# The norm's weights of queries and keys multiplied into the rotation's tables, first 16-head stage

## The reference, cut to what matters

```python
def rmsnorm(x, w, eps=1e-06):
    v = jnp.mean(x * x, axis=-1, keepdims=True)
    return w * (x * jax.lax.rsqrt(v + eps))

h = modulate(rmsnorm(x, norm1_w), sh_msa, sc_msa)
qkv = (h @ qkv_w.T).reshape(B, N, 3, H, D)          # H = 16, D = 16
q = rmsnorm(q, q_norm_w)                            # weights: 16 values for q, 16 for k
k = rmsnorm(k, k_norm_w)
q_r, k_r = apply_rope3d(q[..., :12], k[..., :12], positions)   # pairs (t0, t1) ->
                                                    # (t0*cos - t1*sin, t0*sin + t1*cos)
q = jnp.concatenate([q_r, q[..., 12:]], axis=-1)    # values 12 to 15 are not rotated
k = jnp.concatenate([k_r, k[..., 12:]], axis=-1)
attn = softmax(einsum("bnhd,bmhd->bhnm", q, k) * D ** -0.5)
x = x + g_msa * (einsum("bhnm,bmhd->bnhd", attn, v) @ proj_w.T + proj_b)
```

## Time and profile before

| | |
|---|---|
| median of 3 runs | 2146.8 us (2143.79 to 2148.41) |
| the profiled execution | 2146.22 us, its span 2144.4 us |
| busy shares of the span | PE 89%, DVE 62%, ACT 46%, POOL 38% |
| mean granted clock of TensorE | 0.958 of full speed |
| layer 1's attention | from 856.4 to about 1194 us of the span |

### The profile page before, as it was taken

How to read it: one execution, slowest core, us unless ns; L and a number is a source line. 1 busy time by engine, 2 the same in 40 slices (tenths; PEclk the granted TensorE clock), 3 DMA queues, 4 the chain that set the end, 5 groups by cost and what they waited for, 6 DMA issues and landing times. The chain is left out here.

```text
span 2144.4 us, 44671 instructions
## 1 busy us (share of the span) xinstructions
PE 1917.3 (89%) x17318; PEld 1484.1 (69%) x17318; DVE 1335.8 (62%) x2028; ACT 995.1 (46%) x1693; POOL 819.1 (38%) x731
## 2 busy tenths in 40 slices
PE   6999999999979997788878899978999799988898
PEld 4777777877867775566666677756777677766675
DVE  4454555455545554698888577767988655554455
ACT  3433443444346665455555333324555466643222
POOL 1220211021113444677778233456778633340000
PEclk8999999999989999799998999989999999998999
DMA  5100000000020000100000000010000000003222
GB/s 192 59 2 2 2 2 2 2 2 2 2 65 1 0 0 3 43 2 3 2 1 1 27 0 0 0 40 2 2 0 2 6 25 0 0 12 101 82 70 79
DMA packets 26172, 44.97 MB, mean 21 GB/s; under 512 B 3984, under 2 KB 11984, under 8 KB 25872
## 3 DMA queue, kind: packets, MB, share of 16 engines
q1 hardware_dynamic: 24720, 42.26, 5.9%
q10 hardware_dynamic: 1280, 0.23, 0.1%
HBM read 36.18 MB, written 6.29 MB: 20 GB/s over the span
## 5 line engine op out<-in xcount | busy, mean ns | idle before, releaser
L1203 DVE TENSOR_TENSOR Glb<-Gfb,Ghb 128x512 fp32r<-128x512 f32 x176 | 165.2, 948 | 97.6 <-ACT Ghb L1154 95.9
L441 PE MATMUL bank<-HH,W1b 128*128 128x512 f32 x448 | 184.8, 412 | 16.1 <-PEq L1483 7.2
L323 POOL TENSOR_TENSOR Tm<-Dv,MOD 128x512 f32<-128x512 f32 x94 | 108.5, 1174 | 228.1 <-DVE Dv L380 157.2
L443 PE MATMUL bank<-HH,W1b 128*128 128x512 f32 x448 | 177.1, 395 | 0.0
L442 PE MATMUL bank<-HL,W1b 128*128 128x512 f32 x448 | 176.8, 395 | 0.0
L441 PE MATMUL O<-Ghb,W2b 128*128 128x512 f32 x352 | 143.0, 406 | 36.7 <-DVE Glb L1203 36.7
L461 POOL TENSOR_TENSOR spare<-RT 128x1 f32<-128x1 f32 x32 | 6.5, 202 | 404.3 <-DVE RT L452 404.3
L312 POOL TENSOR_TENSOR XS<-Tm 128x512 f32<-128x512 f32 x48 | 69.5, 1448 | 218.8 <-ACT Tm L278 213.9
L1360 PE MATMUL bank<-WQKa,HH 128*128 128x512 f32 x256 | 97.2, 465 | 47.5 <-DVE HL L388 26.0
L443 PE MATMUL O<-Ghb,W2b 128*128 128x512 f32 x352 | 138.0, 392 | 0.0
L442 PE MATMUL O<-Glb,W2b 128*128 128x512 f32 x352 | 137.7, 391 | 0.0
(11 more groups left out here) (259 smaller groups left out, 5211.7 us busy)
## 6 DMA issues: line engine op xcount, KB each, us to landing
w<-l_w_dram SPq DMA_DIRECT2D x33, 256.0 KB, 3.4
X<-xT_dram SPq DMA_DIRECT2D x16, 256.0 KB, 6.7
out_dram<-XO SPq DMA_DIRECT2D x8, 512.0 KB, 2.8
wm<-w_mods_dram SPq DMA_DIRECT2D x4, 768.0 KB, 5.3
W2b_f<-l_w_dram SPq DMA_DIRECT2D x11, 256.0 KB, 5.1
WQK_f<-l_wqk_dram SPq DMA_DIRECT2D x8, 256.0 KB, 8.9
W1b_0f<-l_w_dram SPq DMA_DIRECT2D x8, 256.0 KB, 3.7
wm<-w_mods_dram SPq DMA_DIRECT2D x4, 384.0 KB, 6.5
```

The costliest lines, as they stand in the source:

```text
L323: nc.gpsimd.tensor_tensor(Tm[:, k].rearrange("p (b t) -> p b t", t=T), Dv[:, k].rearrange("p (b t) -> p b t", t=T), m, ALU.mult).then_inc( ...
L441: nc.tensor.matmul(out, w_lo_ap, x_hi, start=first, stop=False)
L443: return nc.tensor.matmul(out, w_hi_ap, x_hi, start=False, stop=last)
L1203: nc.vector.tensor_tensor(Gl[m % gb][:], gf, Gh[m % gb][:].bitcast(F32), ALU.subtract).then_inc(g_lo.h, 1)
```

## The change

`WN` is no longer multiplied onto the scaled queries and keys. Instead the stage ahead builds two tables per token, `TWc` and `TWs` (32 tiles x {q, k} x 12 values), cosines times weight and signed sines times the partner's weight, and a row `W4` of 4 values, the product of the q and k weights of the values that aren't rotated. In the stage `RA` and `RB` read these tables (an access of four dimensions: partition, q or k, head, value), and the queries' last 4 values are multiplied by `W4` in an instruction on 128 x 16 x 4; the keys' last 4 stay unweighted (a score is a sum of products q*k, so the weight may sit on either). The tables are made by six POOL instructions in `fills`.

To make room, the values' weights `WV` move into the front's region, into the place of `V3`, which goes: the norm's refinement now works in place in `V1`. It has the same instructions and sizes as before. `WN` shrinks to 2 x 16 values, and its DMA with it.

```diff
@@ def dve_norm
-nc.vector.scalar_tensor_tensor(out=V3[:], in0=V2[:], scalar=-0.5, in1=V2[:], op0=ALU.mult, op1=ALU.mult).then_inc(f_n1.h, 1)
+nc.vector.scalar_tensor_tensor(out=V1[:], in0=V1[:], scalar=-0.5, in1=V2[:], op0=ALU.mult, op1=ALU.mult).then_inc(f_n1.h, 1)
...
-nc.vector.tensor_tensor(V3[:], V3[:], V1[:], ALU.mult).then_inc(f_n2.h, 1)
+nc.vector.tensor_tensor(V1[:], V1[:], V2[:], ALU.mult).then_inc(f_n2.h, 1)
...
@@ def fills (attention12_plan)
+if l == 1:
+    pool.wait_ge(d_in.h, d_in.at(n_d))
+    w = WN[:, :, 0:12].rearrange("p s (a i) -> p s a i", i=2)
+    tc, ts = st.TW
+    nc.gpsimd.tensor_tensor(tc[:], rope_c1[:].unsqueeze(2).to_broadcast([P, NT, 2, 12]),
+                            WN[:, :, 0:12].unsqueeze(1).to_broadcast([P, NT, 2, 12]), ALU.mult).then_inc(tw_in.h, 1)
+    for s in range(2):
+        for i in range(2):
+            nc.gpsimd.tensor_tensor(ts[:, :, s].rearrange("p t (a i) -> p t a i", i=2)[:, :, :, i],
+                                    rope_s1[:].rearrange("p t (a i) -> p t a i", i=2)[:, :, :, i],
+                                    w[:, s, :, 1 - i].unsqueeze(1).to_broadcast([P, NT, 6]), ALU.mult).then_inc(tw_in.h, 1)
+    nc.gpsimd.tensor_tensor(st.W4[:], WN[:, 0, 12:DH1], WN[:, 1, 12:DH1], ALU.mult).then_inc(tw_in.h, 1)
@@ def pool_rope
-nc.gpsimd.tensor_tensor(q[:], q[:], WN[:], ALU.mult).then_inc(qk_w.h, 1)
-pool.wait_ge(qk_w.h, qk_w.at(tt + 1))
 n = 12
-cs = rope_c1[:, bass.ds(tt, 1), :].to_broadcast([P, 2 * H, n])
...
+cs = TWc[:, bass.ds(tt, 1)].rearrange("p o s d -> p (o s) d").unsqueeze(2).to_broadcast([P, 2, H, n])
+sn = TWs[:, bass.ds(tt, 1)].rearrange("p o s d -> p (o s) d")
+halves = [(ev(bv)[:, :, :, :, i], ev(qv)[:, :, :, :, 1 - i],
+           sn.rearrange("p s (a i) -> p s a i", i=2)[:, :, :, i].unsqueeze(2).to_broadcast([P, 2, H, n // 2])) for i in range(2)]
+halves.append((q[:, 0:H, n:DH1], q[:, 0:H, n:DH1], W4[:].unsqueeze(1).to_broadcast([P, H, DH1 - n])))
...
-nc.gpsimd.tensor_tensor(RA[:, :, 0:n], q[:, :, 0:n], cs, ALU.mult).then_inc(ra.h, 1)
+nc.gpsimd.tensor_tensor(av, qv, cs, ALU.mult).then_inc(ra.h, 1)
 for o, a, s_ in halves:
     nc.gpsimd.tensor_tensor(o, a, s_, ALU.mult).then_inc(rb.h, 1)
...
-nc.gpsimd.tensor_tensor(q[:, :, 0:n], RA[:, :, 0:n], RB[:, :, 0:n], ALU.add).then_inc(rc.h, 1)
+nc.gpsimd.tensor_tensor(qv, av, bv, ALU.add).then_inc(rc.h, 1)
```

More of the change, by code:

```diff
@@ L108, in cond_stack_kernel @@
             count(n) for n in ("t4_ps", "sq_sb", "ss_sum", "ss_ln", "ss_exp", "ss_n1", "ss_n2", "ss_r")]
-        qk_n, qk_w, ra, rb, rc, tr_free0, tr_free1 = [
-            count(n) for n in ("qk_n", "qk_w", "ra", "rb", "rc", "tr_free0", "tr_free1")]
+        qk_n, tw_in, ra, rb, rc, tr_free0, tr_free1 = [
+            count(n) for n in ("qk_n", "tw_in", "ra", "rb", "rc", "tr_free0", "tr_free1")]
         tr_free = [tr_free0, tr_free1]
@@ L225, in cond_stack_kernel @@
         Tm = FRONT.take("Tm", [P, DH, CH])
-        V1, V2, V3 = [FRONT.take(f"V{i}", [P, CH]) for i in range(3)]
+        V1, V2 = [FRONT.take(f"V{i}", [P, CH]) for i in range(2)]
+        WV_AT = FRONT.off
+        FRONT.off += DH * 2 * P * 4
         H32 = [FRONT.take(f"H32_{i}", [P, DH, CH]) for i in range(2)]
@@ L1286, in attention12_plan @@
             WO = st.WO = res.take(f"WO{tag}", [P, DH, D])
[L1287 to L1290, removed]
+            WV = st.WV = place("WV" + tag, [P, DH, 2, P], WV_AT)
+            if l == 1:
+                WN = st.WN = res.take("WN" + tag, [P, 2, DH1])
+                W4 = st.W4 = res.take("W4" + tag, [P, DH1 - 12])
+                st.TW = [res.take(f"TW{tag}{n}", [P, NT, 2, 12]) for n in "cs"]
+                VBI = RC = st.VBI = st.RC = None
+            else:
+                WN = st.WN = res.take("WN" + tag, [P, 2 * H, DH1])
+                VBI = st.VBI = res.take("VBI" + tag, [P, PAIRS, DH1])
+                RC = st.RC = res.take("RC" + tag, [P, 2, DH1])
             VB = st.VB = [res.take(f"VB{tag}{i}", [P, 2, PAIRS, 2, DH1 + 1]) for i in range(TL)]
@@ L1438, in pool_rope @@
                     if l == 1:
-                        nc.gpsimd.tensor_tensor(q[:], q[:], WN[:], ALU.mult).then_inc(qk_w.h, 1)
-                        pool.wait_ge(qk_w.h, qk_w.at(tt + 1))
                         n = 12
-                        cs = rope_c1[:, bass.ds(tt, 1), :].to_broadcast([P, 2 * H, n])
[L1443 to L1446, removed]
+                        h4 = lambda v: v.rearrange("p (s h) d -> p s h d", s=2)
+                        ev = lambda v: v.rearrange("p s h (a i) -> p s h a i", i=2)
+                        qv, av, bv = h4(q[:])[:, :, :, 0:n], h4(RA[:])[:, :, :, 0:n], h4(RB[:])[:, :, :, 0:n]
+                        cs = TWc[:, bass.ds(tt, 1)].rearrange("p o s d -> p (o s) d").unsqueeze(2).to_broadcast([P, 2, H, n])
[3 more added lines that the diff above has]
+                        halves.append((q[:, 0:H, n:DH1], q[:, 0:H, n:DH1], W4[:].unsqueeze(1).to_broadcast([P, H, DH1 - n])))
                     else:
                         n = DH1
+                        qv, av, bv = q[:], RA[:], RB[:]
                         cs = RC[:, 0:1, :].to_broadcast([P, 2 * H, n])
@@ L1784, in attention12 @@
                 ka_sb.passed(NT); kd_sb.passed(NT)
-                for c in (pt_ps, pt_sb, rb):
+                for c in (pt_ps, pt_sb):
                     c.passed(2 * NT)
+                rb.passed((3 if l == 1 else 2) * NT)
                 if l == 1:
-                    for c in (qk_w, sq_sb, ss_sum, ss_ln, ss_exp, ss_n1, ss_n2, ss_r):
+                    tw_in.passed(6)
+                    for c in (sq_sb, ss_sum, ss_ln, ss_exp, ss_n1, ss_n2, ss_r):
                         c.passed(NT)
```

17 lines of the change are left out of this document (13 added, 4 removed).

## The result

| kernel | median us | lowest to highest | runs |
|---|---|---|---|
| before | 2146.4 | 2143.8 to 2148.4 | 4 |
| after | 2124.6 | 2124.4 to 2128.6 | 4 |

The ratio is 0.9904, with a 95% interval of 0.9888 to 0.9921: the changed kernel is about 1% faster, some 21 us. The forecast was 2133.5 us with a range from 2125.5 to 2143.5. The direction came as predicted and the size did not: some 21 to 22 us instead of 13. The profiled execution of the changed kernel took 2128.6 us, with a span of 2126.8; it is the slowest of the four.

A forecast was written before the change was run, and what follows sets the result against it. Bound: a loop through PE and DVE, whose two-input instructions POOL's hold. (a) to (e) less the tables: 3.6 + 5.0 + 1.8 + 3.0 + 0.8 - 1.1 = 13.1 us, so 2133.5 us; range 2125.5 to 2143.5.

The forecast's parts named there:

- The likeliest case: Whole kernel: gains (a) to (e) less the tables' loss, 13.1 us, giving 2133.5 us; chance 0.50.
- (d): Projection behind PE's wait for `HL`: shorter waits keep the clock in four chunks, weighted 6 of 10; gain 3.0 us.
- (e): End of the stage: the last tile's transposes wait less for the rotation; gain 0.8 us.
- rival 2: DVE's holds and PE's clock: all holds go and the clock stays in all four chunks; 19 us, 2127.5; chance 0.13.
- The rotation: POOL's rotation per tile: product and wait removed, small product of 0.38 us added; net 1.0 us shorter.
- (a): Norm at t = 3: L374 freed, L372 held about 0.3; gain 0.45 per chunk, 8 chunks, 3.6 us.
- (b): Small operations at t = 1: POOL's addition comes earlier, L1419 held 0.6 instead of 1.5; five chunks, gain 5.0 us.
- (c): L388 under POOL's rotation: held 0.3 instead of 0.8; gain 0.45 in five chunks, together 1.8 us.
- The tables: Six POOL instructions in `fills`, 4.6 to 4.7 us, partly in idle time; loss 1.1 us.
- Rival 1: DVE's holds move, half of (a) to (c) returns, clock kept once or never; 5 to 6 us, 2140.5; chance 0.20.
- Rival 3: DVE's holds are hidden in its wait for the square; only (e) and the tables remain, 2147; chance 0.12.
- Rival 4: POOL's four-dimensional products cost extra time, making the kernel slower; 2153 at 1.4 us more; chance 0.05.

The follow-up runs named there:

- e1: Changed kernel plus an unused POOL product on 128x440, reading SBUF, behind each tile's rotation; 2135.9 us, ratio to before 0.9951.
- e5: Changed kernel plus one unused DVE reduction of 0.94 us, one SBUF input, ahead of `HL` in chunks 1 to 7; 2128.9 us, ratio to before 0.9928.
- e8: Changed kernel with the product on 128x512 back and the old tables read, new tables still built but unused; 2147.0 us, ratio to before 1.001.
- e6: Changed kernel plus two unused DVE reductions of 0.94 us each ahead of `HL` in chunks 1 to 7; 2141.6 us, ratio to before 0.9982.
- e4: Changed kernel with the six table-building instructions one chunk earlier in the stage ahead; 2126.3 us, ratio to before 0.9904.
- e3: Changed kernel plus two POOL memsets (0.57 and 0.27 us), which only write, behind each tile's rotation; 2129.8 us, ratio to before 0.9921.
- e2: Changed kernel plus an unused POOL product on 265 values per partition, reading SBUF, behind each tile's rotation; 2129.6 us, ratio to before 0.9914.

## Why the prediction was right, and where its sizes were off

The direction, the place and the path were right: holds inside DVE's instructions, `HL` behind them, PE behind `HL`. The likeliest case gave 13.1 us, the traces show 22.8. The sizes were off in one direction, (d) and (e) most. That the result by its ratio still lies in the range is owed to rival 2 and not to the likeliest sum, and in part to luck, for the clock's terms differ between executions of one kernel. By the steps of the prediction:

**The rotation.** "1.0 us shorter" should have been 1.55: in the loop 5.20 became 3.65. The prediction contradicts itself here, for its own times (sum from 2.9 to 3.9, where 5.2 was the end) are 1.3 shorter. The 0.3 between the two are the sum's: it took 1.36 in the kernel before, where L372 had begun 0.21 us ahead of it and held it, and takes 1.03 now. The other 0.25: the small product took 0.31, not 0.38; the gap of 0.1 ahead of the first product did not come; and the instructions overlap by some hundredths each.

**(a)** was mis-sized: 0.45 per chunk, measured 0.64 to 0.73, about its upper bound of 0.70; 5.5 us instead of 3.6. I let the sum move under L372 and hold it 0.3. It ended 0.13 us behind the start of L374 (the former L372) and held nothing: the group's mean is 695 ns. e1 gave this term back in seven of the eight intervals, 4.1 us.

**(b)** came about as priced, if a little larger: the hold of L1445 went from 1.49 to 0.40 us in such a chunk, and its mean to 260 ns (0.30 us was forecast).

**(c)** was mis-sized: `HL` went from 1.99 to 1.26, 0.7 in such a chunk where 0.45 was counted, and its mean to 1301 (near 1500 was forecast). That is 3.9 us over the stage instead of 1.8. The first half of `RB` does lie at its start, as the prediction says, but has only 0.18 us to run when L390 begins, and L390 took 1.26 where its shortest is 1.21: a hold of 0.05, not 0.3.

**(d)** was mis-sized most. In the four borders inside the stage the traces show 11.8 us where (b), (c) and (d) without the last chunk's gave 4.0 + 1.8 + 3.0 = 8.8. DVE's rows there give 4.4 for (b) and 2.8 for (c), which leaves 4.6 for (d), of an upper bound of 5.1. I gave the clock 6 of 10 and it was kept at every chunk's first projection from chunk 2 on. In e5 it stayed at waits of 1.3 to 1.7 us, so the 1.17 left by (b) and (c) had more margin than I thought. But the term is no sure gain: in e8 the waits were long and the clock stayed in most chunks.

**(e)** left out the clock altogether, and so mis-sized the tail most. The tail became 5.1 us shorter, where 0.8 for the transposes and 1.0 for the fifth L1419 were counted. Those two were right: up to the last tile's transposes the tail is 1.9 us shorter. The other 3.2 lie behind them, 21.4 us before and 18.2 now, and are the stretch at 0.50, which the windows of the kernel before show and which I had not read beyond the first projections. The holds alone don't make it: e1 has the last one back (1.51 us) and a wait of 1.97 for the masking, its clock stays at 1.00, and it too needs 18.2 us behind the transposes. The eight traces with a shorter rotation need 18.2 to 18.6 there, but for e6's 20.2; the two with the long one, where PE waits for it (1.19 us before, 1.85 in e8), need 21.4 and 21.1. So the stretch went with the long rotation; what sets it off isn't shown, for in the kernel before the clock had fallen ahead of that wait.

**Not counted:** 1.3 us at the stage's start and in tile 30.

**The tables** cost 0.96 us, 1.1 was forecast; e4 shows that they are this term. POOL's timeline of the changed kernel at the border, which answers to the earlier trace rows:

```profile
853.16 1.84 POOL L1328 TENSOR_TENSOR TWa1c<-rope_c,WNa 128x768 f32<-128x768 f32 x1
854.96 2.57 POOL L1332 TENSOR_TENSOR TWa1s<-rope_s,WNa 128x192 f32<-128x192 f32 x4
857.49 0.20 POOL L1335 TENSOR_TENSOR W4a<-WNa 128x4 f32<-128x4 f32 x1
```

1.84 + 2.57 + 0.20 = 4.61 us, the 4.6 that the straight line through 384 and 512 values had given.

The differences add up: 1.9 for (a), 3.0 at the borders, 3.3 in the tail, 1.3 not counted, 0.1 for the tables, together 9.6 of the 9.7 us.

**Rivals.** Rival 2, all holds gone and the clock kept, with 19 us and 13%, was the nearest; its terms for the holds and the clock were about right and its tail too small. Rival 1, holds that move, is nearest to what e1 makes of the kernel, 2135.9 (its own sum of 5 to 6 us gives 2141 to 2142, not 2140.5). Rival 3, hidden anyway, falls by e5: 6.6 us of DVE time cost 5.6. Rival 4 falls by e8. The range from 2125.5 ended just above the median, because its lower end was rival 2, which has 1 us for the tail.

## What to carry to other kernels

Where GpSimd and VectorE both read SBUF, look at minimum, median and maximum of each small two-input VectorE instruction: a hold shows as a long instruction and never as a wait, and work that is removed from an idle GpSimd is worth what of it lay under such instructions. Holds come in chains: an instruction of GpSimd can be held by a VectorE one that began ahead of it and then hold the next, so an overlap that goes can shorten instructions on both engines. When a stretch of PE waiting gets shorter, read the granted clock over everything behind it up to the stage's end, not just at the next matmul.

## What the runs showed of the hardware

- A memset on GpSimd neither held a two-input VectorE instruction nor was held by one (e3: 0.57 us under L375, L377 at 692 ns); a product of 265 values, 0.63 us undisturbed, in the same place lengthened L377 to 961 (e2).
- The hold works in both directions, and the one that began first kept its usual time: e1's pad took 1.41 instead of 0.92 behind a VectorE instruction of 0.69, and `RB`'s pair 2.28 and 2.30 instead of 1.32 behind the subtraction, before and after.
- GpSimd products in the changed kernel and before: 4 values 0.20 us, 64 values 0.31, 192 in pieces of six 0.68, 384 1.02, 512 1.28, 768 1.84. A fourth dimension of the access made no difference (1277 and 1278 ns).
- The granted clock is not a function of the last wait. Behind PE's waits for `HL` of 2.19 us and more, 12 first projections took 1.15 to 1.22 and 10 took 0.72 to 0.74, over the ten traces; behind the 37 shorter ones, up to 1.78 us, it was 0.72 to 0.74 each time.
